# First scan of a four-layer chain: POOL's second and third quarter in one step, Ln and Exp of a block's LayerNorm in two stages

## What is computed

```
# L1: 128 steps of a Runge-Kutta integration, 4 derivatives each
i_couple = tanh(q) @ coupling.T
dq = q - q**3 / 3 - p + drive + i_couple + bias
dp = 0.08 * (q + 0.7 - 0.8 * p)
...                                  # q, p after each step; q is the output
x = x + L1(cond, cond, x)
# L2: LayerNorm over the 256 features, modulated by cond, then the projections
x1  = (x - mean) * rsqrt(var + 1e-6) * (1 + scale1) + shift1
qkv = x1 @ qkv_w + qkv_b
```

## Time and profile before

| | |
|---|---|
| median of 3 runs | 1752.91 us (1749.85 to 1754.81) |
| profiled execution | 1748.66 us |
| its span | 1746.9 us |
| busy TensorE, weight loads | 1397.5 us (80%), 1071.3 us (61%) |
| busy VectorE | 1227.8 us (70%) |
| busy ScalarE | 827.1 us (47%) |
| busy POOL | 315.7 us (18%) |
| mean granted TensorE clock | 0.841 |
| the scan's tanh, first to last | 259 to 926 us |
| table loads in the scan | 6 of 1.283 us |

### The profile page before, as it was taken

One profiled execution on the slowest core, in us unless ns is written; L12 is line 12 of the kernel. 1 busy time (PEld: TensorE's weight loads), 2 busy tenths in 40 slices (PEclk: granted clock), 3 DMA queues, 4 the chain that ended last, 5 costly groups with the idle time before them and its releaser, 6 DMA issues. The chain is left out here.

```text
span 1746.9 us, 47635 instructions
## 1 busy us (share of the span) xinstructions
PE 1397.5 (80%) x16714; PEld 1071.3 (61%) x16714; DVE 1227.8 (70%) x6993; ACT 827.1 (47%) x3110; POOL 315.7 (18%) x616
## 2 busy tenths in 40 slices
PE   6889874445589969995998977888888589999865
PEld 4377643334456646663666866777776367777764
DVE  4357769999999999998995215555554556676754
ACT  3557843332445454554553226555553644444322
POOL 1015521111211121112111022222220301111110
PEclk8979995555579968996998979999999698989855
DMA  3000000110013202320335569566521300000000
GB/s 128 0 1 2 2 22 29 50 50 2 2 62 110 92 32 82 109 92 14 103 107 193 196 205 284 153 167 189 158 84 49 85 1 3 3 12 6 15 15 14
DMA packets 102839, 127.64 MB, mean 73 GB/s; under 512 B 6109, under 2 KB 79433, under 8 KB 97353
## 3 DMA queue, kind: packets, MB, share of 16 engines
q1 hardware_dynamic: 102128, 122.46, 22.6%
q0 software_dynamic: 272, 2.10, 0.6%
q10 hardware_dynamic: 200, 0.05, 0.0%
HBM read 70.06 MB, written 54.53 MB: 71 GB/s over the span
## 5 line engine op out<-in xcount | busy, mean ns | idle before, releaser
L999 PE MATMUL bank<-s_tanh_hi,coup_hi 128*128 128x16 f16 x2048 | 136.6, 176 | 164.3 <-ACT s_tanh_hi L989 163.0
L999 PEld LDWEIGHTS bank<-s_tanh_hi,coup_hi 128*128 128x128 f16 x2048 | 90.3, 102 | 267.2 <-ACT s_tanh_hi L989 262.6
L1476 ACT ACTIVATE prob<-bank,neg_max 128x128 f32<-128x128 f32 x256 | 90.7, 366 | 123.2 <-DVE neg_max L1510 123.2
L910 POOL TENSOR_SCALAR s_p_scaled<-s_p 128x32 f32<-128x32 f32 x128 | 37.5, 293 | 577.1 <-DVE s_p L893 556.0
L999 PE MATMUL bank<-s_tanh_lo,coup_hi 128*128 128x16 f16 x2048 | 136.0, 176 | 2.2
L989 ACT ACTIVATE s_tanh_hi<-s_s 128x32 f16<-128x32 f32 x256 | 58.7, 229 | 163.1 <-DVE s_s L827 158.8
L1522 DVE TENSOR_TENSOR o_lo<-bank,o_hi 128x512 fp32r<-128x512 f32 x64 | 44.3, 692 | 120.8 <-ACT o_hi L1487 120.8
L999 PE MATMUL bank<-s_tanh_hi,coup_lo 128*128 128x16 f16 x2048 | 127.2, 171 | 0.0
L659 PE MATMUL bank<-x_hi,w_hi 128*128 128x512 f32 x256 | 120.6, 471 | 2.5 <-DVE x_lo L1169 2.5
L999 PEld LDWEIGHTS bank<-s_tanh_lo,coup_hi 128*128 128x128 f16 x2048 | 89.1, 101 | 33.1 <-DVE s_tanh_lo L821 0.8
L1756 PE MATMUL bank<-h_hi,w_h_hi 128*128 128x16 f16 x1536 | 91.2, 172 | 21.6 <-DVE h_hi L1974 21.6
(11 more groups left out here) (307 smaller groups left out, 4457.4 us busy)
## 6 DMA issues: line engine op xcount, KB each, us to landing
queries<-tile_stage SPq DMA_DIRECT2D x64, 256.0 KB, 2.3
keys<-tile_stage SPq DMA_DIRECT2D x64, 256.0 KB, 2.3
values<-tile_stage SPq DMA_DIRECT2D x64, 256.0 KB, 2.4
q_raw<-queries SPq DMA_DIRECT2D x16, 1024.0 KB, 9.7
k<-keys SPq DMA_DIRECT2D x16, 1024.0 KB, 12.0
v<-values SPq DMA_DIRECT2D x64, 256.0 KB, 6.4
x<-in_L_cond_qkv_w_dram SPq DMA_DIRECT2D x6, 1024.0 KB, 5.0
x_tok<-in_x_dram SPq DMA_DIRECT2D x4, 512.0 KB, 5.6
```

The costliest lines, as they stand in the source:

```text
L910: G.tensor_scalar(p_scaled, p, P_IN_P, None, MUL).then_inc(pool_done, 1)
L999: ins = nc.tensor.matmul(coupled[:, B * m:B * m + B], w[:, o:o + P], th[:, B * c:B * c + B], start=(first and c == 0 and m == 0), stop=(la ...
L1476: last = A.activation(prob[:, i % PR, h, :], SB[i % 3][:, T * h:T * h + T], ACT.Exp, bias=neg_max[:, i % PR, h:h + 1], accum_out=sums[:, i ...
```

## The change

In `plan`, ScalarE's item "rstd" at r + 25 becomes two: "log" at r + 25, "rstd" at r + 26. The function `root` is cut in two accordingly. In POOL's loop the quarters are distributed over the steps 7, 8 and 9 behind the ready point as (0), (1, 2), (3), before as (0), (1), (2), (3) over the steps 7 to 10. Each quarter keeps its wait and its increment.

```diff
-        for at, item in [(15, ("square", n, 0)), (18, ("square", n, 1)), (25, ("rstd", n))] + [
+        for at, item in [(15, ("square", n, 0)), (18, ("square", n, 1)), (25, ("log", n)), (26, ("rstd", n))] + [
...
-                n, k = divmod(j - TB - 7, TB)
-                if n >= 0 and k < 4:
+                n, at = divmod(j - TB - 7, TB)
+                for k in ((0,), (1, 2), (3,))[at] if n >= 0 and at < 3 else ():
                     pool.wait_ge(xhat_ready, 8 * n + C * k + 2)
                     for b in range(4 * k, 4 * k + 4):
                         last = G.tensor_scalar(xc[:, 1, TB * b:TB * b + TB], xc[:, 1, TB * b:TB * b + TB],
...
-            def root(n):
+            def logarithm(n):
                 act.wait_ge(var_full, 4 * n + 4)
                 A.activation(rstd[:, :], VAR[:, :], ACT.Ln, bias=g.eps6[:, :]).then_inc(log_ready, 1)
+
+            def root(n):
                 act.wait_ge(log_ready, n + 1)
                 A.activation(rstd[:, :], rstd[:, :], ACT.Exp, scale=-0.5).then_inc(rstd_ready, 1)
...
+                elif kind == "log":
+                    logarithm(*of)
```

## The result

The changed kernel took 1738.73 us (median of 6 runs, 1737.14 to 1739.80) against 1753.29 us before (6 runs, 1749.85 to 1754.81): ratio 0.992, interval 0.9906 to 0.9933. Faster by 14.6 us, where 4.6 were forecast. The same changed kernel was measured in two more sessions (a session is one set of runs in which a few kernels take turns with the kernel before).

| session | changed | before | ratio, interval |
|---|---|---|---|
| first | 1738.73 (6 runs) | 1753.29 (6) | 0.992, 0.9906 to 0.9933 |
| second | 1742.06 (6) | 1752.32 (17) | 0.9944, 0.9932 to 0.9956 |
| third | 1749.03 (12) | 1748.10 (23) | 1.0005, 0.9992 to 1.0018 |

What follows compares the result with a forecast made beforehand. No engine was full; the scan's tanh-to-tanh stage length was taken as the bound. Three blocks saving 0.54 + 0.98 us each give 4.6 us off the 1752.91 us median: 1748.3 us, range 1743 to 1753.

Steps and rivals of the forecast that it cites:

- The second load: ScalarE's table load ahead of Exp moves ahead of the next stage's tanh, which starts earlier: gain 0.54 us per block.
- Stage 26: Scan stage that receives Exp, counted from a block's 32 steps being done: still 1.21 us from tanh to tanh.
- The rounding's wait: ScalarE's rounding of chunk 1 no longer waits for POOL's last quarter: gain 0.98 us per block, bounds 0.9 to 1.03.
- the small corrections left out of the sum: At the rounding's stage: VectorE's work ahead gives hundredths back; without POOL it should take 1.45 us, not 1.50.
- Exp is hidden: Exp, 0.63 us behind the tanh pair, runs under TensorE's and VectorE's part of its stage, with 0.3 us to spare.
- POOL's double step: Step 8 of a block, where POOL runs quarters 1 and 2: ends about 475.4, leaving 1.5 us free.
- Rivals 1: A third table load in each block, for Exp after tanh: only 1.9 us gained, 1751.0 us; chance 0.05.
- 4: POOL late in its double step, delaying the scaling of p: 1.5 us per block eats the gain, 1752.9 us; chance 0.02.
- 3 x (0.54 + 0.98) = 4.6 us: Forecast saving in the scan: three blocks, each with ScalarE's 0.54 and POOL's 0.98 us; bounds 4.2 to 4.9.
- What the sum can't fix: TensorE's granted clock where the scan's tile products start: one slow stage more or less per block, 1.8 us in all.
- Rivals 2: Clock rises sooner after the scan's tile products start: two slow stages fewer per block, 3.6 us more gained, 1744.7; chance 0.12.
- 3: Clock rises later after the scan's tile products start: three more slow stages per block, 5.4 us, 1753.7; chance 0.05.

Runs made afterwards that it cites:

- e5: The kernel before, cut behind the first scan with a write of what stood there: 937.34 us.
- e8: The changed kernel, cut behind the keys-and-values phase that follows the scan: 1031.34 us.
- e7: The kernel before, cut behind the keys-and-values phase that follows the scan: 1042.63 us.
- e17: The changed kernel once more, whole and unaltered, in the third session: 1749.03 us, ratio 1.0005 to the kernel before.
- e11: The changed kernel, cut behind the keys-and-values phase, with seventeen idle, waited-for VectorE multiplications late in the scan: 1038.33 us.
- e13: The kernel before, cut behind the keys-and-values phase, with unread filler products in three places of that phase where TensorE has nothing to do: 1037.16 us.
- e2: The kernel before with only POOL's part of the diff, Ln and Exp left together: 1744.76 us, ratio 0.9956.
- e3: The kernel before with only ScalarE's part of the diff, POOL's quarters left in four steps: 1747.34 us, ratio 0.9967.
- e9: The kernel before, cut behind the keys-and-values phase, with ten idle, waited-for VectorE multiplications late in the scan: 1041.27 us.

## Why the prediction was wrong

**Right, to a few hundredths.** The second load moves to the tanh and no third one comes (0.54 forecast, 0.53 to 0.55 measured, three blocks). Stage 26 grew by 0.02 us. The rounding's wait goes entirely (0.98 forecast, with 1.03 as the upper bound; 1.01 to 1.03 measured: the small corrections left out of the sum were real). Exp is hidden; POOL's double step has 1.42 us free where 1.5 were said. Rivals 1 and 4 are out: two loads per block, no wait for the scaling of p. The 3 x (0.54 + 0.98) = 4.6 us are 4.7 in the trace, and the cut kernels have 5.4 for the whole scan.

**Wrong: "What the sum can't fix".** This step put the clock's part at 1.8 us and looked for it in one place, the start of the tile products in the scan, and the sum before it took for granted that the phases behind would be as long as before. The runs showed the next phase shorter by 2.4 us in the first two profiles and by 5.9 in the cut kernels (e5 to e8). In the profiles of e7 and e8 it is TensorE's clock, behind the two pauses (4.2 us) and at the small products (2.4). They also showed a place in the scan worth 2.0 us that I had not priced either (stages 6 to 11). At the tile start itself the clock did what I said: single stages by up to 0.6 us, 0.4 in sum between the first two profiles. The profile before had the row that would have warned, a mean of 0.86 in the same 12 us of the keys-and-values phase, with two pauses in it:

```profile
948.80:960.80 12.00, 9.38 (x34) 7.31 (x35) 4.24 (x9) 3.01 (x7) 2.29 (x7) 0.86 0.56 180
```

Rivals 2 and 3 had the right mechanism at the wrong place. A rival for pauses of TensorE with or without the low clock behind them would have had, by e7 and e8, a price of 6 us of either sign. Around 1748.3 that is 1742.3 to 1754.3 us, which holds the third median, just misses the second and lies 3.6 us above the first.

**Wrong, too: one session taken for the kernel.** The interval of a session holds for that session. The three ratios of the changed kernel, 0.992, 0.9944 and 1.0005, lie outside each other's intervals; the single forecast of 1748.3 us lies between the second and the third median. I can't say which of the three is usual.

**Open.** What sets how a session's executions lie against the clock's changes. The changed kernel's runs of the first session (1737.14 to 1739.80) and of the third (1746.93 to 1751.99) don't even touch. The unfilled pair was not run in the session of the filled one, nor the pair without delay in that of the delays, so the fall's coming and going there may be the session's. In e17 the phase `project0` took 69.0 us where all other profiles of whole kernels have 69.9 to 70.5. But e11 and e13 have 69.0 and 69.1 there without the fall, and e7 has 70.4 with it, so that alone doesn't decide. Also open is how the surplus of the first session, 10 us, divides: its two profiles differ by 8.9 us only, 4.6 of them from the two edits, and the other 5.7 us of the difference of the medians lie in executions that nobody profiled. The cut kernels explain 6.7 us of surplus (11.3 less 4.6), and they ran in another session. That e2 and e3 have their surplus from the same place is argued, not shown: in their profiles that phase has 106.7 us, not shorter than before.

## What to carry to other kernels

The sum over the edited stages is exact where a stage is a closed circle: it came to a few hundredths in every profile, while the whole scan of the changed kernel varied by 3.1 us (661.5 to 664.6). Beside it, look at each pause of TensorE behind the edit, and ask what the clock behind it is in the profile and what the work there would take at the other level; that price, with both signs, belongs in the range of any change that shifts it by some microseconds. And when a change yields more than its stages explain, repeat it in another session before believing the rest, and cut the kernel short on both sides of a phase: the piece's executions spread less than those of the whole (1.5 to 5.0 us against up to 11.8). And run the unchanged piece in the same session as each variant of it; without that a delay or a filler can't be told from the session.

## What the runs showed of the hardware that was not expected

- A change of ScalarE's tables took 1.283 us between instructions that follow each other at 0.01 to 0.02 us (461.52 + 0.69, 462.23, 463.52 in the earlier trace rows), Exp and tanh share tables, and the same load ahead of tanh costs the same.
- A kernel with TensorE work added had 5.5 us less (e7 to e13), and one with VectorE work added on the path 1.4 us less (e7 to e9); these are medians of different sessions and chips, and the additions aren't shown to be the cause.
- The same two pauses of 1.8 and 2.5 us in the same kernel had a mean clock of 1.00 over the 12 us from the first of them in one execution, and of 0.57 in another.
- The low clock costs small products as well: 64 of 128x128 by 128x1 took 8.7 us from first to last in e8 and 11.1 in e7, at a median of 0.250 and 0.352 us each.
- Eight POOL modulations in a row beside VectorE: stage 33 took 1.29 to 1.33 us instead of 1.27 or 1.28.
